# Results written into the memory of the split x, a step's four stores issued by ScalarE, and SyncE's gathers placed around the x loads

## The chip, the cores and the metric

The kernel runs on one core of one Trainium2 chip. The metric is the device time of one execution in microseconds. A core has five instruction streams that matter here: TensorE (PE, with its weight loads shown as PEld), VectorE (DVE), ScalarE (ACT), GpSimd (POOL) and SyncE (SP), and 16 DMA engines that all of them share. In this kernel SP computes nothing: it issues transfers.

## The reference, cut to what matters

The input x has 64 sequences of 64 tokens with 1024 features. Two layers are applied, each of which adds to x what an adapter pair and a feed-forward part with four small experts give:

```
x = x + ffn0(cond0(x))        cond: Bx = x @ B[id].T ; out = Bx @ A[id].T      (rank 16, one id per sequence)
x = x + ffn1(cond1(x))        ffn:  x @ W.T + b + sum_e softmax(router)_e * 2 * (x @ EA_e.T) @ EB_e.T
```

The adapter ids of a sequence choose among 8 (layer 0) and 64 (layer 1) adapters, so the adapter rows are gathered by values that are only known at run time.

## The kernel before, in words

**Tiling.** A step `g` is one of 8 groups of 8 sequences (512 tokens); x and the result are held as 128 partitions x 8 feature tiles x 512 tokens. One step's x is loaded in `CH` = 4 chunks of two feature tiles (512 KB each) into `xraw[par]`, where `par` alternates between two buffers. Every factor of a product is kept as a high part in fp32r and the low remainder: ScalarE copies the high part, DVE or GpSimd subtracts it for the low part, and TensorE runs three products. For x these parts are `xs_hi` and `xs_lo` (`xs[0]`, `xs[1]`): they hold only half of a step's tokens at a time, so they are written twice a step (`split_x`, half 0 and half 1).

**One step on TensorE.** `body(g)` begins with `ps_h` (from `bst`, the split B rows), then the selection `ps_s`, then the wide products W1 x A1 into three banks (`wide(0)`, `wide(1)`, and `wide(2)` in two pieces of four). Between the two pieces of `wide(2)` stands `turn()` (line 447): four transposes of `lp`, the weighted expert coefficients of layer 0, which DVE makes at the end of its `softmax(0)`. Then come `project(g + 1, 0)` and `project(g + 1, 1)`, which multiply the next step's split x, a second `turn()`, and the eight result tiles, each of which DVE adds to x (line 903) with a `d_out` signal.

**What DVE and ScalarE do in the first part of a step.** ScalarE: `h_and_k1(g)` (which first waits for a sum of DVE's), then `split_b(g + 1)` (four copies `bst_hi`), which waits until all 16 gathers of step g + 1 have landed (`gathered`), then `wide_high(0)` (`m1x_hi`), the copies of `ps_t`, and the first chunks of `split_x(g + 1)`. DVE, in the same order: `h_to_sbuf`, `k1_low`, `split_b` (four `bst_lo`), `wide_low(0)`, the `ps_t` parts, and `softmax(0)`, which ends with `lp` (line 855).

**SP's queue.** In `body(g)` SP prepares step g + 2: it waits until POOL has finished `split_a(g + 1)` (`a_lo`), gathers the eight sequences' adapter rows (for each sequence 64 KB at line 233 and 128 KB at line 235), and then for each chunk waits for `d_out`, stores the chunk (line 296), and loads the next x into the chunk before it (line 216) once that chunk's store has landed, since result and x share `xraw[par]`. The engines take instructions in program order; signals are semaphores. Steps 1 to 4 are two turns of a loop on SP, steps 0 and 5 to 7 are written out.

Of the kernel before, what the change touches and what calls it, by code (L numbers as in the profile page):

```python
# [29 lines left out]
P = 128  # L30
# [17 lines left out]
CH = 4  # L48
# [23 lines left out]
def two_layer_adapter_lora(nc, x_in, id0_row, all_ids, a0, b0_tab, ab1_tab, w0, w1, exp0, exp0_rows,  # L72
                           exp1_in, exp1_rows, bias, identity, marks, out):
    with ExitStack() as ctx:
        def sb(name, shape, dt=F32):
            return ctx.enter_context(nc.sbuf_tensor(name, shape, dt))

        def split(name, shape):

            return sb(name + "_hi", shape, F32R), sb(name + "_lo", shape, F32R)  # L80
# [8 lines left out]
        xraw = [sb(f"xraw{i}", [P, KT, TOK]) for i in range(2)]  # L89

        slots = [t[:, KC * i:KC * (i + 1), :].rearrange("p k t -> p (k t)") for t in xraw for i in range(CH)]
        xs = split("xs", [P, KT, HALF])
        abraw = sb("abraw", [P, GROUP, 2, SLOT])
        b0raw = sb("b0raw", [P, GROUP, SLOT])
        bst = split("bst", [P, KT, 4, HR_])
# [30 lines left out]
        bsum = sb("bsum", [P, KT])  # L126

        hr_hi, hr_lo = hr[:, :, 0, :], hr[:, :, 1, :]
        exp1_hi, exp1_lo = (w[:, :, D:WIDE] for w in w1s)

        zs = hsb[:].rearrange("p a n -> p (a n)")[:, 0:TT * FC].rearrange("p (j e c) -> p j e c", j=TT, e=EXP)
# [71 lines left out]
        def result_banks(last):  # L203

            return ps_d + [ps_p, ps_h] if last else ps_d

        def after_step(eng, signal, count):

            if not (isinstance(count, int) and count == 0):
                eng.wait_ge(signal, count)  # L210


        @block.sync
        def _(sp):
            def load_x(g, par, i):
                sp.dma_start(xraw[par][:, KC * i:KC * (i + 1), :],
                             x_in[bass.ds(g, 1), :, KC * i:KC * (i + 1), :]
                             .rearrange("a p k t -> p (a k) t")).then_inc(x_in_sem[i], 16)

            def values(first, count, limit):  # L220

                return nc.values_load_multi_w_load_instructions(
                    ids[0:1, bass.ds(first, count)], (mybir.EngineType.SP,), min_val=0, max_val=limit - 1)[1]

            def pick(g):

                return tuple(zip(values(g * GROUP, GROUP, ADAPT0), values(g * GROUP + SEQS, GROUP, SEQS)))

            def gather(picks, seqs):

                for b in seqs:
                    n0, n1 = picks[b]
                    sp.dma_start(b0raw[:, b, :],  # L233
                                 b0_tab[bass.ds(n0, 1)].rearrange("a p n -> p (a n)")).then_inc(gathered, 16)
                    sp.dma_start(abraw[:, b, :, :].rearrange("p a n -> p (a n)"),  # L235
                                 ab1_tab[bass.ds(n1, 1)].rearrange("a p n -> p (a n)")).then_inc(gathered, 16)

            sp.dma_start(ids[:], all_ids).then_inc(ids_in, 16)
            sp.dma_start(a0raw, a0).then_inc(a0_in, 16)
            for k in range(KT):  # L240
                sp.dma_start(w0raw[k], w0[k]).then_inc(w0_in[k], 16)
            sp.wait_ge(ids_in, 16)
            experts = values(2 * SEQS, EXP, 16)
            for e, n in enumerate(experts):
                sp.dma_start(exp0_raw[:, e, :], exp0[bass.ds(n, 1)].rearrange("a p n -> p (a n)")
                             ).then_inc(exp0_in, 16)
            picks = pick(0)
            sp.dma_start(ident[:], identity).then_inc(ident_in, 16)
            sp.wait_ge(a0_lo, 1)

            for i in range(CH):
                gather(picks, range(2 * i, 2 * i + 2))
                sp.wait_ge(w0_lo, i + 1)
                load_x(0, 0, i)
            sp.dma_start(mark[:], marks).then_inc(marks_in, 16)
            sp.dma_start(idi[:], id0_row).then_inc(marks_in, 16)
            for k in range(KT):
                if W1_SLOTS[k] in W1_SLOTS[:k]:

                    sp.wait_ge(w1_lo, max(j for j in range(k) if W1_SLOTS[j] == W1_SLOTS[k]) + 1)  # L260
                elif W1_SLOTS[k] == SPARE:
                    sp.wait_ge(m0t_done, 1)
                else:
                    sp.wait_ge(w0_lo, W1_SLOTS[k] + 1)
                sp.dma_start(w1raw[k], w1[k]).then_inc(w1_in[k], 16)
                if k == 2:
                    sp.dma_start(exp1_raw.rearrange("p k c -> p (k c)"), exp1_in).then_inc(exp1_sem, 16)
                    sp.dma_start(bia[:], bias).then_inc(exp1_sem, 16)
                    picks = pick(1)
                if k == 6:  # L270
                    sp.wait_ge(w1_lo, 4)
                    for e, n in enumerate(experts):
                        r0 = E0ROWS[0].start + e * ER
                        sp.dma_start(rows_raw[r0:r0 + ER, :],
                                     exp0_rows[bass.ds(n, 1)].rearrange("a r o -> (a r) o")
                                     ).then_inc(rows_in, 16)
                    sp.dma_start(rows_raw[E1ROWS[0], :], exp1_rows).then_inc(rows_in, 16)
            sp.wait_ge(b_lo, 4)
            sp.wait_ge(a_lo, 1)
            gather(picks, range(GROUP))  # L280
            sp.wait_ge(w1_lo, KT - 1)
            sp.wait_ge(w1_lo_pool, 1)
            for i in range(CH - 1):
                load_x(1, 1, i)
            sp.wait_ge(rows_lo, 2)
            load_x(1, 1, CH - 1)

            def body(g, par, last):
                ahead = not (isinstance(g, int) and g >= STEPS - 2)
                if ahead:  # L290
                    picks = pick(g + 2)
                    sp.wait_ge(a_lo, g + 2)
                    gather(picks, range(GROUP))
                for i in range(CH):
                    sp.wait_ge(d_out, KT * g + KC * (i + 1))
                    sp.dma_start(out[bass.ds(g, 1), :, KC * i:KC * (i + 1), :]
                                 .rearrange("a p k t -> p (a k) t"),
                                 xraw[par][:, KC * i:KC * (i + 1), :]).then_inc(stored[i], 16)
                    if ahead and i > 0:
                        sp.wait_ge(stored[i - 1], 16 * g + 16)  # L300
                        load_x(g + 2, par, i - 1)
                if ahead:
                    sp.wait_ge(stored[CH - 1], 16 * g + 16)
                    load_x(g + 2, par, CH - 1)

            steps(sp, body, 3)
            for i in range(CH):
                sp.wait_ge(stored[i], 16 * STEPS)


        @block.tensor
# [206 lines left out]
        def _(act):  # L518
            def copy(dst, src):
                return act.activation(dst, src, ACT.Copy)  # L520

            def split_x(g, par, half, chunks=range(CH)):
                n = 2 * g + half
                for i in chunks:
                    act.wait_ge(x_in_sem[i], 16 * g + 16)
                    if not (isinstance(n, int) and n == 0):
                        act.wait_ge(x_used, CH * n + (i + 1 - CH))
                    copy(xs[0][:, KC * i:KC * (i + 1), :],
                         xraw[par][:, KC * i:KC * (i + 1), half * HALF:(half + 1) * HALF]).then_inc(x_hi, 1)

# [83 lines left out]
            def body(g, par, last):  # L614
# [60 lines left out]
                if not last:  # L675
                    c0_high(g + 1)

            steps(act, body)


        @block.vector
        def _(dve):
# [113 lines left out]
            def body(g, par, last):  # L796
# [102 lines left out]
                banks = result_banks(last)  # L899

                for m in range(KT):
                    dve.wait_ge(d_done, KT * g + m + 1)
                    dve.scalar_tensor_tensor(out=xraw[par][:, m, :], in0=banks[m % len(banks)][:],  # L903
                                             scalar=bsum[:, m:m + 1], in1=xraw[par][:, m, :],
                                             op0=ALU.add, op1=ALU.add).then_inc(d_out, 1)
                    if not last and m == 1:
                        select(g + 1)
                    if not last and m == 2:
                        c0_low(g + 1)
# [5 lines left out]
        def _(pool):  # L915
            def low(dst, whole, high):
                return pool.tensor_tensor(dst, whole, high.bitcast(F32), ALU.subtract)  # L917

            def split_x(g, par, half, chunks):
                for i in chunks:  # L920
                    pool.wait_ge(x_hi, 2 * CH * g + CH * half + i + 1)
                    low(xs[1][:, KC * i:KC * (i + 1), :],
                        xraw[par][:, KC * i:KC * (i + 1), half * HALF:(half + 1) * HALF],
                        xs[0][:, KC * i:KC * (i + 1), :]).then_inc(x_lo, 1)
# [82 lines left out]
```

## Time and profile before

| | us |
|---|---|
| median of 3 runs | 353.43 (350.32 to 354.69) |
| the profiled execution | 353.02 |
| its span in the profile | 351.0 |
| TensorE busy | 326.0 (93%) |
| DVE busy | 246.0 (70%) |
| ScalarE busy | 149.8 (43%) |
| GpSimd busy | 89.9 (26%) |

The profile's page divides the span into 40 slices of 8.8 us. TensorE's digit there is 9 in nearly all slices after the first 80 us; the DMA digits swing between 0 and 9 within every step. In the chain that ended last, TensorE's work makes up 53% of the span. An engine's idle time matters only where TensorE waits for its result. Times below are from the span's start.

### The profile page before, as it was taken

To read this page: it belongs to the slowest core of one execution; us is meant where nothing else is said; L and a number is where in the kernel's file an instruction comes from. 1 tells how busy PE (TensorE), PEld (TensorE's weight loads), DVE (VectorE), ACT (ScalarE), POOL (GpSimd) and SP (SyncE) were. 2 spreads that over 40 slices of the span, in tenths; PEclk is the share of its full clock that TensorE was granted. 3 is DMA by queue.
4 is the path that set the end of the run, shared out by engine and by line. 5 is a ranking of instruction groups with operands and counts; after the bars stand their busy time and mean duration, and the time that the engine had idled before them with its cause. 6 is when DMAs were issued, how large, how long until landed. Compare 5 with 4: busy or idle time off the path is not lost.

```text
span 351.0 us, 6577 instructions
## 1 busy us (share of the span) xinstructions
PE 326.0 (93%) x2112; PEld 304.6 (87%) x2112; DVE 246.0 (70%) x496; ACT 149.8 (43%) x317; POOL 89.9 (26%) x61
## 2 busy tenths in 40 slices
PE   6998747889999999999999999999999999999975
PEld 5777647879999899989999999999999999999864
DVE  5925993797586867697668767775878586855554
ACT  5856833663065405550456036613562166203210
POOL 0014620184015500550046003620262026300000
PEclk9999898969999999999999999999999999999989
DMA  6889526611782078405950586048803780140005
GB/s 276 327 278 326 181 92 203 219 58 51 250 269 92 17 228 287 132 2 166 302 189 0 143 289 225 0 120 268 266 5 98 245 296 18 49 190 2 0 23 218
DMA packets 31525, 56.17 MB, mean 160 GB/s; under 512 B 3793, under 2 KB 21074, under 8 KB 31506
## 3 DMA queue, kind: packets, MB, share of 16 engines
q1 hardware_dynamic: 31506, 55.94, 47.9%
q8 instruction: 9, 0.15, 0.2%
q14 instruction: 10, 0.08, 0.1%
HBM read 39.15 MB, written 16.78 MB: 159 GB/s over the span
## 4 chain that ended last, share of the span: by engine, by line
PE 53%; issue 12%; DMA 10%; DVE 9%; POOL 6%; SPq 5%; ACT 4%; POOLq 0%; ACTq 0%; DVEq 0%
PE ps_d L316 12%; PE ps_d L318 12%; PE ps_d L317 12%; POOL xs_lo L917 5%; DMA xraw<-w 4%; DMA out<-xraw 3%; PE ps_h L323 3%; PE ps_p L316 2%; DVE k_lo L684 2%; PE ps_p L317 2%; PE ps_p L318 2%; PE ps_t L447 2%; DMA abraw<-ab_tab 2%; SPq L233 2%; SPq L235 2%
## 5 line engine op out<-in xcount | busy, mean ns | idle before, releaser
L917 POOL TENSOR_TENSOR xs_lo<-xraw,xs_hi 128x512 fp32r<-128x512 f32 x48 | 67.8, 1423 | 195.4 <-ACT xs_hi L520 195.3
L316 PE MATMUL ps_d<-w1s_hi,a1s_hi 128*128 128x384 f32 (+1 forms) x216 | 72.7, 337 | 1.8 <-DVE w1s_lo L684 1.8
L318 PE MATMUL ps_d<-w1s_hi,a1s_lo 128*128 128x384 f32 (+1 forms) x216 | 70.2, 325 | 0.0
L317 PE MATMUL ps_d<-w1s_lo,a1s_hi 128*128 128x384 f32 (+1 forms) x216 | 70.2, 325 | 0.0
L903 DVE SCALAR_TENSOR_TENSOR xraw<-ps_d,bsum,xraw 128x512 f32<-128x512 f32 x62 | 46.3, 750 | 27.5 <-PE ps_d L318 27.5
L520 ACT ACTIVATE xs_hi<-xraw 128x512 fp32r<-128x512 f32 x64 | 38.4, 624 | 17.6 <-DMA xraw<-x_in 11.1
L316 PEld LDWEIGHTS ps_d<-w1s_hi,a1s_hi 128*128 128x128 f32 x216 | 41.1, 190 | 3.9 <-DVE w1s_lo L684 3.8
L316 PE MATMUL ps_p<-xs_hi,bst_hi 128*128 128x256 f32 x128 | 39.4, 307 | 3.4 <-POOL xs_lo L917 2.5
L317 PEld LDWEIGHTS ps_d<-w1s_lo,a1s_hi 128*128 128x128 f32 x216 | 41.1, 190 | 0.0
L318 PEld LDWEIGHTS ps_d<-w1s_hi,a1s_lo 128*128 128x128 f32 x216 | 41.0, 190 | 0.0
L317 PE MATMUL ps_p<-xs_lo,bst_hi 128*128 128x256 f32 x128 | 37.8, 295 | 0.0
L318 PE MATMUL ps_p<-xs_hi,bst_lo 128*128 128x256 f32 x128 | 37.7, 295 | 0.0
L316 PE MATMUL ps_d<-k_hi,m1x_hi 128*128 128x256 f32 x124 | 35.8, 289 | 1.4 <-DVE k_lo L684 1.4
L520 ACT ACTIVATE hsb<-hsb 128x32 f32<-128x32 f32 x8 | 1.8, 228 | 82.3 <-DVE hsb L704 82.3
L318 PE MATMUL ps_d<-k_hi,m1x_lo 128*128 128x256 f32 x124 | 35.6, 287 | 0.0
L317 PE MATMUL ps_d<-k_lo,m1x_hi 128*128 128x256 f32 x124 | 35.5, 286 | 0.0
L316 PEld LDWEIGHTS ps_p<-xs_hi,bst_hi 128*128 128x128 f32 x128 | 26.3, 205 | 4.9 <-issue 2.0
L684 DVE TENSOR_TENSOR m1x_lo<-ps_d,m1x_hi 64x384 fp32r<-64x384 f32 (+1 forms) x48 | 24.4, 509 | 5.9 <-ACT m1x_hi L520 5.1
L316 PEld LDWEIGHTS ps_d<-k_hi,m1x_hi 128*128 128x128 f32 x124 | 24.0, 194 | 3.6 <-DVE k_lo L684 1.6
L317 PEld LDWEIGHTS ps_p<-xs_lo,bst_hi 128*128 128x128 f32 x128 | 26.3, 206 | 0.0
L318 PEld LDWEIGHTS ps_p<-xs_hi,bst_lo 128*128 128x128 f32 x128 | 26.2, 204 | 0.0
L520 ACT ACTIVATE m1x_hi<-ps_d 64x384 fp32r<-64x384 f32 (+1 forms) x48 | 21.3, 444 | 11.0 <-PE ps_d L318 10.6
(156 smaller groups left out, 691.8 us busy)
## 6 DMA issues: line engine op xcount, KB each, us to landing
xraw<-x_in SPq DMA_DIRECT2D x32, 512.0 KB, 5.0
out<-xraw SPq DMA_DIRECT2D x32, 512.0 KB, 3.6
xraw<-w SPq DMA_DIRECT2D x16, 512.0 KB, 6.5
abraw<-ab_tab SPq DMA_DIRECT2D x64, 128.0 KB, 2.1
b0raw<-b_tab SPq DMA_DIRECT2D x64, 64.0 KB, 1.9
b0raw<-a SPq DMA_DIRECT2D x1, 512.0 KB, 3.7
lp<-exp SPq DMA_DIRECT2D x4, 69.0 KB, 7.5
cm<-exp_in SPq DMA_DIRECT2D x1, 144.0 KB, 5.3
```

The source lines that it names most:

```text
L233: sp.dma_start(b0raw[:, b, :], b0_tab[bass.ds(n0, 1)].rearrange("a p n -> p (a n)")).then_inc(gathered, 16)
L235: sp.dma_start(abraw[:, b, :, :].rearrange("p a n -> p (a n)"), ab1_tab[bass.ds(n1, 1)].rearrange("a p n -> p (a n)")).then_inc(gathered, 16)
L316: pe.matmul(acc, lh, rh, start=first, stop=False, skip_group_check=True)
L317: pe.matmul(acc, lh, rl, start=False, stop=False, skip_group_check=True)
L318: return pe.matmul(acc, ll, rh, start=False, stop=final, skip_group_check=True)
L323: pe.matmul(acc, high, right.rearrange("p a n -> p (a n)"), start=first, stop=False, skip_group_check=True)
L447: mm = pe.transpose(ps_t[:, j * P:(j + 1) * P], lp[:, at:at + P], ident[:])
L520: return act.activation(dst, src, ACT.Copy)
L684: return dve.tensor_tensor(dst, whole, high.bitcast(F32), ALU.subtract)
L903: dve.scalar_tensor_tensor(out=xraw[par][:, m, :], in0=banks[m % len(banks)][:], scalar=bsum[:, m:m + 1], in1=xraw[par][:, m, :], op0=ALU. ...
L917: return pool.tensor_tensor(dst, whole, high.bitcast(F32), ALU.subtract)
```

## The change

Three things are altered. **First**, the result tiles get memory of their own: `done`, 16 KB per partition, allocated over the address of `xs_hi` and `xs_lo`. Its four chunks lie as two over `xs_hi` and two over `xs_lo`. DVE's line that adds the result now writes `done` in place of `xraw`. So an x chunk of step g + 2 can be loaded when DVE has read the old x (`d_out`), without waiting for a store; and what writes `xs` next (ScalarE for `xs_hi`, GpSimd for `xs_lo`, the first half of the following step's `split_x`) first waits for the stores of what lies there. **Second**, the four stores are issued by ScalarE, at the end of its `body`. **Third**, SP issues the first four gathers, then chunk 0 of x, two gathers, chunk 1, two gathers, chunk 2, chunk 3.

```
+        xs_at = nc.sbuf_base
         xs = split("xs", [P, KT, HALF])
+        done_ = nc.alloc_sbuf_tensor_at("done", [P, KT * TOK], F32, offset=xs_at)
...
+        done = [done_[:, KC * TOK * i:KC * TOK * (i + 1)] for i in range(CH)]
...
+        def stored_by(g):
+            return 0 if isinstance(g, int) and g == 0 else 16 * g - 16
...
@@ sync, body
-                    gather(picks, range(GROUP))
-                for i in range(CH):
-                    sp.wait_ge(d_out, KT * g + KC * (i + 1))
-                    sp.dma_start(out[bass.ds(g, 1), :, KC * i:KC * (i + 1), :]
-                                 .rearrange("a p k t -> p (a k) t"),
-                                 xraw[par][:, KC * i:KC * (i + 1), :]).then_inc(stored[i], 16)
-                    if ahead and i > 0:
-                        sp.wait_ge(stored[i - 1], 16 * g + 16)
-                        load_x(g + 2, par, i - 1)
-                if ahead:
-                    sp.wait_ge(stored[CH - 1], 16 * g + 16)
-                    load_x(g + 2, par, CH - 1)
+                    gather(picks, range(HSEQ))
+                    for i in range(CH):
+                        sp.wait_ge(d_out, KT * g + KC * (i + 1))
+                        load_x(g + 2, par, i)
+                        if i < 2:
+                            gather(picks, range(HSEQ + 2 * i, HSEQ + 2 * i + 2))
...
@@ scalar, split_x
+                    if half == 0:
+                        after_step(act, stored[i // KC], stored_by(g))
...
@@ scalar, end of body
+                for i in range(CH):
+                    act.wait_ge(d_out, KT * g + KC * (i + 1))
+                    act.dma_start(out[bass.ds(g, 1), :, KC * i:KC * (i + 1), :]
+                                  .rearrange("a p k t -> p (a k t)"), done[i]).then_inc(stored[i], 16)
...
@@ vector, results
+                    if last and m % KC == 0:
+                        dve.wait_ge(stored[m // KC], 16 * g)
                     dve.wait_ge(d_done, KT * g + m + 1)
-                    dve.scalar_tensor_tensor(out=xraw[par][:, m, :], in0=banks[m % len(banks)][:],
+                    dve.scalar_tensor_tensor(out=done[m // KC][:, m % KC * TOK:(m % KC + 1) * TOK],
+                                             in0=banks[m % len(banks)][:],
...
@@ gpsimd, split_x
+                    if half == 0:
+                        after_step(pool, stored[KC + i // KC], stored_by(g))
```

The waits for the end of the last stores move from SP to ScalarE. Nothing changes on TensorE.

On SP, in the loop's first turn before, this is the end of the gathers (`b0raw`, `abraw`) and what follows them, with the stores (`out<-xraw1`) and the x loads (`xraw1<-x_in`); ISA and REGISTER_ALU rows prepare addresses and wait values:

```order
L233 DMA b0raw<-b0_tab 128x128
L235 ISA
L235 DMA abraw<-ab1_tab 128x256
L295 ISA
L296 ISA
L296 DMA out<-xraw1 128x1024
L295 REGISTER_ALU
L296 ISA
L296 DMA out<-xraw1 128x1024
L300 ISA
L216 ISA
L216 DMA xraw1<-x_in 128x1024
```

And this is the same stretch of SP now, from the fourth sequence's gathers over the first x load and the fifth and sixth:

```order
L243 DMA abraw<-ab1_tab 128x256
L303 ISA
L224 ISA
L224 DMA xraw1<-x_in 128x1024
L241 ISA
L241 DMA b0raw<-b0_tab 128x128
L243 ISA
L243 DMA abraw<-ab1_tab 128x256
```

Four of a step's eight pairs of gathers now stand behind one or two x loads; none did before. On ScalarE, the last of the four stores at a step's end and the beginning of the next step, as it is now; the rows of lines 681 and 682 are new, and before this the copy `c0s_hi` was followed by the address row and the copy `hsb`:

```order
L681 REGISTER_ALU
L682 ISA
L682 DMA out<-done_49 128x1024
L543 REGISTER_ALU
L520 ACTIVATE hsb<-hsb 128x32
L520 ACTIVATE k1_hi<-ps_s 128x512
L534 ISA
L520 ACTIVATE bst_hi<-abraw 128x4x8x16
```

The row of line 534 is the address of the `split_b` copies, which wait for the gathers; it stands where it stood.

## Rows read from the trace of the kernel before

**Rows 1.** Windows, one steady step: us, busy of each engine, PEclk, DMA share, GB/s

```profile
184.70:220.90 36.20, 35.89 (x249) 34.22 (x249) 26.59 (x57) 15.16 (x36) 10.70 (x8) 1.00 0.49 159
```

**Rows 2.** Timeline of ScalarE: start, us, instruction [idle before]; a step's first copy

```profile
133.75 0.23 ACT L520 ACTIVATE hsb<-hsb 128x32 f32<-128x32 f32 x1 [11.75 <-DVE hsb L704]
...
170.57 0.23 ACT L520 ACTIVATE hsb<-hsb 128x32 f32<-128x32 f32 x1 [11.76 <-DVE hsb L704]
...
206.78 0.23 ACT L520 ACTIVATE hsb<-hsb 128x32 f32<-128x32 f32 x1 [11.75 <-DVE hsb L704]
```

**Rows 3.** Timeline of ScalarE in that step, from split_b to the last first-half chunk

```profile
207.53 0.62 ACT L520 ACTIVATE bst_hi<-abraw 128x512 fp32r<-128x512 f32 x1
...
210.42 0.99 ACT L520 ACTIVATE m1x_hi<-ps_d 64x384 fp32r<-64x384 f32 x2 [0.71 <-PE ps_d L318]
...
212.21 1.14 ACT L520 ACTIVATE xs_hi<-xraw 128x512 fp32r<-128x512 f32 x2
...
219.04 0.63 ACT L520 ACTIVATE xs_hi<-xraw 128x512 fp32r<-128x512 f32 x1 [0.33 <-DMA xraw<-x_in]
```

**Rows 4.** Timeline of VectorE in that step, behind its split_b

```profile
210.94 1.15 DVE L684 TENSOR_TENSOR m1x_lo<-ps_d,m1x_hi 64x384 fp32r<-64x384 f32 x2 [0.18 <-ACT m1x_hi L520]
212.34 0.29 DVE L684 TENSOR_TENSOR c0s_lo<-ps_t,c0s_hi 128x128 fp32r<-128x128 f32 x1 [0.25 <-ACT hls_hi L520]
...
216.38 0.29 DVE L855 TENSOR_TENSOR lp<-hsb,lg 128x128 f32<-128x128 f32 x1
```

**Rows 5.** Waits, 193 to 229.2 us, then 112 to 330 us: total us, times, longest

```profile
PEld ps_t L447 <- DVE lp L855: 0.2, 1, 0.2
...
ACT xs_hi L520 <- DMA xraw<-x_in: 5.2, 8, 1.6
```

**Rows 6.** Timeline of VectorE, a step's first two and last result tiles

```profile
195.16 1.47 DVE L903 SCALAR_TENSOR_TENSOR xraw<-ps_d,bsum,xraw 128x512 f32<-128x512 f32 x2 [0.79 <-PE ps_d L318]
...
203.68 0.75 DVE L903 SCALAR_TENSOR_TENSOR xraw<-ps_d,bsum,xraw 128x512 f32<-128x512 f32 x1 [0.67 <-PE ps_d L318]
```

**Rows 7.** Timeline of SyncE's queue: first and last gather, first and later x loads

```profile
193.96 0.34 SPq L233 DMA_DIRECT2D b0raw<-b_tab  x1
...
201.69 0.33 SPq L235 DMA_DIRECT2D abraw<-ab_tab  x1
...
205.28 0.35 SPq L216 DMA_DIRECT2D xraw<-x_in  x1
...
211.53 2.98 SPq L216 DMA_DIRECT2D xraw<-x_in  x2
```

**Rows 8.** The page's DMA issues: KB each, median us from issue to landing

```profile
xraw<-x_in SPq DMA_DIRECT2D x32, 512.0 KB, 5.0
...
abraw<-ab_tab SPq DMA_DIRECT2D x64, 128.0 KB, 2.1
b0raw<-b_tab SPq DMA_DIRECT2D x64, 64.0 KB, 1.9
```

**Rows 9.** Windows without engine columns: us, PEclk, DMA share, GB/s

```profile
3.00:14.00 11.00, 1.00 1.02 412
...
19.00:25.00 6.00, 1.00 0.90 278
...
194.00:197.10 3.10, 1.00 0.40 122
...
208.00:213.00 5.00, 1.00 0.97 361
```

**Rows 10.** The chain that ended last: start, us, what; the first step's last gather

```profile
24.60 5.62 DMA abraw<-ab_tab
```

**Rows 11.** Windows of TensorE alone: us, PE busy, PEclk, DMA share, GB/s

```profile
57.00:58.00 1.00, 0.00 (x0) 1.00 0.66 202
...
69.00:71.00 2.00, 0.12 (x1) 1.00 0.35 94
72.00:78.00 6.00, 5.31 (x24) 0.50 0.04 15
```

More of the change, by code:

```diff
@@ L292, in body @@
                     sp.wait_ge(a_lo, g + 2)
-                    gather(picks, range(GROUP))
-                for i in range(CH):
-                    sp.wait_ge(d_out, KT * g + KC * (i + 1))
-                    sp.dma_start(out[bass.ds(g, 1), :, KC * i:KC * (i + 1), :]
-                                 .rearrange("a p k t -> p (a k) t"),
-                                 xraw[par][:, KC * i:KC * (i + 1), :]).then_inc(stored[i], 16)
-                    if ahead and i > 0:
-                        sp.wait_ge(stored[i - 1], 16 * g + 16)
-                        load_x(g + 2, par, i - 1)
-                if ahead:
-                    sp.wait_ge(stored[CH - 1], 16 * g + 16)
-                    load_x(g + 2, par, CH - 1)
+                    gather(picks, range(HSEQ))
[4 more added lines that the diff above has]
+                            gather(picks, range(HSEQ + 2 * i, HSEQ + 2 * i + 2))
             steps(sp, body, 3)
-            for i in range(CH):
-                sp.wait_ge(stored[i], 16 * STEPS)
         @block.tensor
@@ L676, in body @@
                     c0_high(g + 1)
+                for i in range(CH):
+                    act.wait_ge(d_out, KT * g + KC * (i + 1))
+                    act.dma_start(out[bass.ds(g, 1), :, KC * i:KC * (i + 1), :]
+                                  .rearrange("a p k t -> p (a k t)"), done[i]).then_inc(stored[i], 16)
             steps(act, body)
+            for i in range(CH):
+                act.wait_ge(stored[i], 16 * STEPS)
         @block.vector
```

## The prediction, made before the changed kernel was run

> **What bounds the kernel now.** I read the windows of one steady step first, then the waits, then the timelines of ScalarE, VectorE and SyncE over that step, and last the windows of the DMA engines. In a steady step TensorE is busy for 35.89 of 36.20 us at the full clock [rows 1]: a step is as long as TensorE's work, and the change takes none of it away. What can be won is only what TensorE waits for in connection with x. The first copies of two steps are 36.82 us apart (133.75 to 170.57), those of the next 36.21 (170.57 to 206.78) [rows 2]. The long one is the step in which x came late. ScalarE waited for x for 5.2 us in 8 places [rows 5], but most of that lies under TensorE's work: apart from the 0.6 us of the long step nothing of it reaches a step's length. So the gain to be had is about 0.7 us in all.
>
> What can be lost hangs on a narrower chain. DVE ends `lp` at 216.38 + 0.29 = 216.67 [rows 4], and TensorE waits for it before `turn()`, by 0.2 us already [rows 5]. Behind its four `bst_lo`, DVE idles only 0.18 us before `m1x_lo` and 0.25 us before `c0s_lo` [rows 4]. So when `split_b` comes late by more than 0.43 us, `lp` is late by the rest, and TensorE, which takes its instructions in order, stands still for as long. `split_b` starts at 207.53, directly behind ScalarE's earlier work and with no wait for a DMA [rows 3]: the gathers are in memory then. The last is issued at 201.69 [rows 7] and takes 2.1 us to land [rows 8], so they are there at about 203.8, 3.7 us early. That slack is what the change spends.
>
> **The change, part by part.**
>
> *The results' memory.* DVE's 64 result instructions keep shape and operands from the same memories; I cost them at nothing (0.75 us each as now [rows 6]). In the last step DVE has four more waits, for stores issued a step ago: nothing.
>
> *ScalarE issues 32 stores.* No row shows a DMA issue on ScalarE. SP's issue of one takes 0.33 to 0.35 us in the rows of its queue [rows 7], the slowest kind there 1.49 (2.98 for two, which held a wait in it). The last result tile ends at 203.68 + 0.75 = 204.43 [rows 6], and ScalarE's next work starts at 206.78 [rows 2], after 11.75 us of idling. Behind the last wait stands one issue: done at 204.8, or at 205.9 with the dear price. ScalarE's copies behind it are on time either way: 0, and not below 0, since nobody waits for these instructions. Queued behind the waits for `d_out` are exactly those copies, and the gap is the cover.
>
> *The new waits of ScalarE and GpSimd for the stores.* They stand before the first-half chunks of x, the earliest at 212.21 [rows 3], and the stores of the lower half of `done` are issued from 196.7 on (195.16 + 1.47 [rows 6]). At 212.21 ScalarE needs the first store and GpSimd, just behind it, the third; both are issued before the last gather, which lands at about 209.3 (worked out below): 0. In the last step the stores are issued by ScalarE behind the same last tile as by SP now: 0.
>
> *x earlier.* SP issues x chunk 0 at about 198.3 and not at 205.28, the last two at about 203.7 and 204.6 and not from 211.53 on [rows 7]. The needs are at 212.21 for the first and 219.04 for the last [rows 3]. The late x disappears: -0.7 us in all.
>
> *The gathers later.* This is the term that decides. SP's gathers start at 193.96 and go out at 0.52 us each (201.69 - 193.96 over 15). In the new order four pairs are out at 198.1, x chunk 0 follows, two pairs, chunk 1, two pairs: the last gather goes out at about 203.2, 1.5 us later than now. In front of it or beside it the engines now have eight pairs (192 KB each [rows 8], 1.57 MB), two x loads and, from 196.7 on, three stores (512 KB each, 2.62 MB): 4.19 MB. Before, only the gathers were there. Until 197.1 the trace of today moves 122 GB/s x 3.1 us = 0.38 MB [rows 9]. The other 3.81 MB take 9.2 us at 412 GB/s, the best rate of a queue of large transfers; 10.6 us at 361, the rate of x loads and stores mixed; 13.7 us at 278, the rate of gathers mixed with x loads [rows 9]. I take 350 GB/s, since two thirds of the bytes are large transfers: 10.9 us, to 208.0. From the last byte to the signal I add 1.3 us, an estimate: of a gather's 2.1 us [rows 8], 0.33 is the issue and about 0.5 its own bytes. The gathers are all there at 209.3. A second row agrees in kind: in the first step SP issued gathers and x loads in just such a mix, and the last gather, issued at 24.60, landed 5.62 us later [rows 10]; 203.2 + 5.6 is 208.8, without stores beside it.
>
> So `split_b` starts at 209.3 and not 207.53, 1.77 us late; less 0.43 of slack TensorE loses 1.34 us. The lateness comes back in every step, because SP's start hangs on `a_lo` and on `d_out`, which move with TensorE. The gathers of body 0 to 5 feed `split_b` of six steps: 6 x 1.34 = +8.0 us. Between its ends the term is 0 (412 GB/s: 206.3 + 1.3 = 207.6, within the slack; a gain is excluded, as `split_b` does not wait for gathers now) and 6 x 4.1 = +24.9 us (278 GB/s: 210.8 + 1.3 = 212.1, 4.57 late, less 0.43). What is late next is nothing new: with TensorE shifted, all later waits of the step shift too.
>
> **The sum.** -0.7 + 8.0 = +7.3 us on the profiled execution's 353.02, so 360.3; the median of the runs shown is 0.4 us above that execution, so I write 360.7. That is 2.1% over the median, and 2%, about what a measurement of this kernel can tell from no change, is 7.1 us.
>
> **How the DMA engines share their time** is not in this trace: all transfers are SP's. The sum above serves bytes as they come. The Trainium skill (DMA: Bandwidth & Descriptors, section Queues, rings and completion order) says that each of two issuing engines has its own ring on each DMA engine and that a DMA engine takes turns between rings that have work, a packet at a time. No run here shows it; by that rule the sum would be the second rival's, +18.8 us. The same page (Issuing engines are not separate DMA queues) says that issuing on two engines adds no bandwidth, which speaks against this change; the sum already counts all transfers against one rate.
>
> **Rivals.**
>
> *The gathers still land in time* (not slower). Place: ScalarE's `split_b`; price: nothing but the 0.7 us won. It decides below a landing at 208.0, that is at 395 GB/s or more after 197.1. For it: 412 GB/s has been moved for 11 us on end [rows 9], and a store beside a load may fill what a load alone leaves idle. Against it: the mixed rate of 361, and the 5.62 us of [rows 10]. Time: 353.4 - 0.7 = 352.7.
>
> *The stores take half of the engines.* From 197.1 SP's own queue holds 1.19 MB of gathers and 1.05 MB of x up to its last gather; at half of 350 GB/s that is 12.8 us, to 209.9, and the signal at 211.2: 3.67 late, 3.24 lost, six times 19.5, less 0.7: +18.8, so 372.2. For it: the stores' queue has work nearly all that time. Against it: the two queues carry much the same number of bytes, so that first-come and half-and-half differ only by the fourth store and by the time it starts.
>
> *TensorE's clock falls after each new stall.* Between 69 and 71 us TensorE is busy for 0.12 us, and its granted clock is 0.50, the 1.2 GHz level, from 72 to 78 [rows 11]. Against it: it idled from 57 to 58 us at a clock of 1.00 [rows 11], and a stall of 1.3 us is nearer to that. Were each of six stalls followed by 3 us, half of what [rows 11] show, at half the clock, 1.5 us of work would be lost each time: +9.0 on top of 7.3, so 369.7.
>
> *A gain that tells.* It would need 7.1 us, while all idle time of TensorE in seven steady steps is some 7 x 0.31 us [rows 1] and the late x. I see no mechanism.
>
> **How the numbers follow.** Gathers late by the sum's mechanism 0.45, spread from +1 to +16 us around +7.3, about 0.25 of it over 2% and 0.20 under; in time 0.27; half of the engines 0.13; the clock 0.12; a telling gain 0.03. Slower 0.25 + 0.13 + 0.12 = 0.50, within 2% 0.20 + 0.27 = 0.47, faster 0.03. Since the cases of both kinds hold most of the chance, the likeliest one's own range is 354 to 369. The full range goes down to 351, the case in time with the spread of the runs (350.32 to 354.69), and up to 374, which takes in the half share and the clock; the 24.9 us end stays out, with less than 0.1.
>
> **What would show it.** In the changed trace: ScalarE's first `bst_hi` of steps 1 to 6 with idle time put down to a gather's DMA, about 1.8 us (right), or none (the first rival); TensorE's wait before line 447 for `lp` at 1.3 to 1.6 us a step and not 0.2; steps 37.5 us long and not 36.2; `xs_hi` waiting for x no more; the DMA share near 1 from 197 to 212 us of that step, and then low. A granted clock under 1.00 in the steady steps would speak for the third rival. I am wrong if the step keeps 36.2 us, or if ScalarE's `hsb` copy comes late behind its stores.

## The result, and the profile after

The changed kernel takes 381.64 us (median of 4 runs, 380.24 to 385.74) against 353.37 us: ratio 1.083, 95% interval 1.072 to 1.094. It is 28 us slower. The forecast of 360.7 us had the direction, but the time lies above the range of 351 to 374.

The profiled execution took 380.24 us with a span of 378.1. The page's lines of TensorE and of the DMA engines by slice:

```profile
PE 332.4 (88%) x2112; PEld 309.6 (82%) x2112; DVE 242.8 (64%) x496; ACT 149.5 (40%) x317; POOL 88.8 (23%) x61
DMA  7897437308900493008900690049301960032005
```

TensorE runs the same 2112 products and is busy 6.4 us longer, with 88% of the span instead of 93%. The DMA engines now alternate between full slices and empty ones: a step's transfers have been pushed together. ScalarE's timeline over the same part of a step as in [rows 2, 3] (start, us, instruction, idle before it and who ended it), one step further on in the program's time:

```profile
211.15 8.17 ACTq L682 DMA_DIRECT2D out<-done  x4
221.14 0.23 ACT L520 ACTIVATE hsb<-hsb 128x32 f32<-128x32 f32 x1 [11.75 <-DVE hsb L713]
...
225.70 0.63 ACT L520 ACTIVATE bst_hi<-abraw 128x512 fp32r<-128x512 f32 x1 [3.71 <-DMA abraw<-ab_tab]
```

The four stores end before `hsb`, which again follows after 11.75 us of idling: issuing them costs ScalarE's work nothing. `split_b`, which followed `hsb` and `k_hi` without a wait in [rows 3], now waits 3.71 us for gathers. The waits of the six steps behind the start, 90 to 345 us (total, times, longest):

```profile
ACT bst_hi L520 <- DMA abraw<-ab_tab: 24.3, 6, 5.0
PE ps_t L447 <- DVE lp L864: 19.9, 6, 4.3
```

Every one of six `split_b` is late, by 24.3 us together, and TensorE stands still before `turn()` for 19.9 us of it. SyncE's queue in this step, as in [rows 7]:

```profile
208.35 0.34 SPq L241 DMA_DIRECT2D b0raw<-b_tab  x1
...
212.59 0.55 SPq L224 DMA_DIRECT2D xraw<-x_in  x1
...
215.43 0.86 SPq L243 DMA_DIRECT2D abraw<-ab_tab  x1
216.54 0.39 SPq L224 DMA_DIRECT2D xraw<-x_in  x1
...
218.91 0.33 SPq L243 DMA_DIRECT2D abraw<-ab_tab  x1
219.49 0.91 SPq L224 DMA_DIRECT2D xraw<-x_in  x2
```

The last gather goes out 10.56 us after the first (218.91 - 208.35) and not 7.73 as before. It has landed 17.35 us after the first was issued (225.70). What the DMA engines did meanwhile (us, PEclk, DMA share, GB/s):

```profile
208.35:212.00 3.65, 1.00 0.41 127
212.00:217.00 5.00, 1.00 0.93 261
217.00:225.70 8.70, 1.00 1.04 400
```

And what TensorE did behind the late `split_b` (us, PE busy, PEclk, DMA share, GB/s):

```profile
221.20:231.20 10.00, 9.96 (x67) 1.00 0.60 235
231.20:234.30 3.10, 0.16 (x1) 1.00 0.00 0
234.30:237.60 3.30, 3.30 (x13) 0.52 0.00 0
237.60:261.90 24.30, 23.99 (x169) 1.00 0.43 136
```

It is dense, then idle for 3 us, then works 3.3 us at a granted clock of 0.52, the 1.2 GHz level, then dense again at 2.4 GHz.

**Where the 28 us are.** Over the six steps from the second `hsb` copy to the last, the time went from 217.94 us (97.42 to 315.36 in the trace of before) to 246.56 (97.38 to 343.94): +28.6. The windows of TensorE over exactly these six steps, before and then after, tell the kinds apart (us, PE busy, PEclk, DMA share, GB/s):

```profile
97.42:315.36 217.94, 215.58 (x1484) 1.00 0.48 156
```

```profile
97.38:343.94 246.56, 224.83 (x1484) 0.96 0.38 136
```

The same 1484 products in the records took 224.83 us instead of 215.58: 9.3 us for the slower clock. TensorE's idle time grew from 2.36 to 21.73, by 19.4: the stalls are 19.9, and elsewhere it idles 0.5 us less. The two make up the 28.6. Outside these steps the new span is 1.5 us shorter.

### The profile page after: what moved, and what is told of

It is laid out like the page before. It is cut to its first block, busy times and chain, and to the rows that moved or that the text cites. A ratio compares the mean times of both kernels' runs of the same rounds, so it can differ in the third digit from the quotient of the medians.

```text
span 378.1 us, 6659 instructions
## 1 busy us (share of the span) xinstructions
PE 332.4 (88%) x2112; PEld 309.6 (82%) x2112; DVE 242.8 (64%) x496; ACT 149.5 (40%) x317; POOL 88.8 (23%) x61
## 4 chain that ended last, share of the span: by engine, by line
issue 20%; PE 19%; DMA 16%; SPq 15%; POOL 12%; DVE 9%; ACT 7%; POOLq 0%; ACTq 0%
DMA abraw<-ab_tab 13%; POOL xs_lo L929 9%; SPq L241 6%; SPq L243 6%; PE ps_d L316 4%; PE ps_d L318 4%; PE ps_d L317 4%; DMA xraw<-w 4%; ACT bst_hi L520 3%; POOL a1s_lo L929 3%; SPq L224 2%; DVE w1s_lo L693 2%; DVE xs_lo L693 1%; DVE bst_lo L693 1%; PE ps_p L316 1%
## 5 line engine op out<-in xcount | busy, mean ns | idle before, releaser
L316 PE MATMUL ps_d<-w1s_hi,a1s_hi 128*128 128x384 f32 (+1 forms) x216 | 76.5, 354 | 3.2 <-DVE w1s_lo L693 3.2
L318 PE MATMUL ps_d<-w1s_hi,a1s_lo 128*128 128x384 f32 (+1 forms) x216 | 73.3, 339 | 0.0
L317 PE MATMUL ps_d<-w1s_lo,a1s_hi 128*128 128x384 f32 (+1 forms) x216 | 73.2, 339 | 0.0
L914 DVE SCALAR_TENSOR_TENSOR done<-ps_d,bsum,xraw 128x512 f32<-128x512 f32 x62 | 46.1, 749 | 26.1 <-PE ps_d L318 26.1
L316 PEld LDWEIGHTS ps_d<-w1s_hi,a1s_hi 128*128 128x128 f32 x216 | 44.1, 204 | 5.7 <-DVE w1s_lo L693 5.4
L317 PEld LDWEIGHTS ps_d<-w1s_lo,a1s_hi 128*128 128x128 f32 x216 | 43.8, 203 | 0.0
L318 PEld LDWEIGHTS ps_d<-w1s_hi,a1s_lo 128*128 128x128 f32 x216 | 43.4, 201 | 0.0
L520 ACT ACTIVATE xs_hi<-xraw 128x512 fp32r<-128x512 f32 x64 | 37.1, 620 | 13.3 <-PE ps_p L318 8.2
L447 PE MATMUL ps_t<-ident,lp 128*128 128x128 f32 x64 | 11.4, 306 | 21.0 <-DVE lp L864 21.0
L693 DVE TENSOR_TENSOR bst_lo<-abraw,bst_hi 128x512 fp32r<-128x512 f32 x16 | 12.6, 786 | 24.6 <-ACT bst_hi L520 24.6
L447 PEld LDWEIGHTS ps_t<-ident,lp 128*128 128x128 f32 x64 | 7.8, 150 | 23.4 <-DVE lp L864 23.3
```

The lines of the kernel that those rows point to most:

```text
L316: pe.matmul(acc, lh, rh, start=first, stop=False, skip_group_check=True)
L317: pe.matmul(acc, lh, rl, start=False, stop=False, skip_group_check=True)
L318: return pe.matmul(acc, ll, rh, start=False, stop=final, skip_group_check=True)
L447: mm = pe.transpose(ps_t[:, j * P:(j + 1) * P], lp[:, at:at + P], ident[:])
L693: return dve.tensor_tensor(dst, whole, high.bitcast(F32), ALU.subtract)
L914: dve.scalar_tensor_tensor(out=done[m // KC][:, m % KC * TOK:(m % KC + 1) * TOK], in0=banks[m % len(banks)][:], scalar=bsum[:, m:m + 1], i ...
```

## The experiments

All ratios are to the kernel before, timed beside each kernel on the same chip; its median was 351.5 to 353.4 us on the chips used, so the ratios compare better than the times. "Wait" is what ScalarE waited for gathers in the six steps, in all; "stall" is TensorE's idle time before `turn()` in the same six steps. The kernel before has none of either there.

| | time, us | ratio (95%) | wait | stall |
|---|---|---|---|---|
| the change | 381.64 | 1.083 (1.072 to 1.094) | 24.3 | 19.9 |
| gathers first | 352.23 | 0.999 (0.996 to 1.002) | 1.0 | 0.3 |
| order of the change, stores on SyncE | 364.41 | 1.028 (1.021 to 1.035) | 14.2 | 10.0 |
| no stores | 351.68 | 0.998 (0.995 to 1.001) | 1.0 | none |
| x chunks 2 and 3 held | 380.03 | 1.078 (1.072 to 1.083) | 24.1 | 19.7 |
| filler products | 373.40 | 1.061 (1.056 to 1.066) | 24.9 | 4.2 |
| fourth store late | 366.78 | 1.043 (1.038 to 1.048) | 16.4 | 12.1 |
| third and fourth store late | 356.90 | 1.013 (1.008 to 1.018) | 8.9 | 4.8 |
| x chunk 1 behind the gathers | 361.80 | 1.030 (1.023 to 1.037) | 11.0 | 6.8 |
| own memory alone | 352.96 | 1.005 (1.001 to 1.009) | none | 1.4 |
| order alone | 384.18 | 1.093 (1.084 to 1.102) | 26.6 | 21.6 |

### Gathers first

```
-                    gather(picks, range(HSEQ))
+                    gather(picks, range(GROUP))
                     for i in range(CH):
                         sp.wait_ge(d_out, KT * g + KC * (i + 1))
                         load_x(g + 2, par, i)
-                        if i < 2:
-                            gather(picks, range(HSEQ + 2 * i, HSEQ + 2 * i + 2))
```

> The changed kernel with one part undone: SyncE issues all eight pairs of gathers ahead of the four x loads, as before the change; results' own memory and the stores on ScalarE stay. Theory (the x loads in front of the last gathers make them late): split_b waits for no DMA or under 0.5 us, steps are 36.2 us long, the time is 352 to 355 us. Rival (the stores on a second queue take the engines from the gathers, whatever SyncE's order): split_b still waits 1.5 us or more in each of six steps, and the time is above 362 us.

Measured 352.23 us, as expected. ScalarE waited once in six steps, for 1.0 us where under 0.5 was expected:

```profile
ACT bst_hi L518 <- DMA abraw<-ab_tab: 1.0, 1, 1.0
```

With the order of before, results' own memory and ScalarE's stores cost nothing that can be measured, and they win nothing either. Putting the gathers back ahead of the x loads takes the whole 28 us away. The rival, that the second queue by itself takes the engines from the gathers, is out.

### The order of the change with the stores on SyncE

```
                     gather(picks, range(HSEQ))
-                    for i in range(CH):
-                        sp.wait_ge(d_out, KT * g + KC * (i + 1))
+                for i in range(CH):
+                    sp.wait_ge(d_out, KT * g + KC * (i + 1))
+                    sp.dma_start(out[...], done[i]).then_inc(stored[i], 16)
+                    if ahead:
                         load_x(g + 2, par, i)
                         if i < 2:
                             gather(picks, range(HSEQ + 2 * i, HSEQ + 2 * i + 2))
```

and no stores on ScalarE.

> The changed kernel with the stores issued by SyncE again, each ahead of the x load of its chunk and of the two pairs of gathers behind it; results' own memory and the place of the gathers stay, so that all transfers are in one queue. If what stands ahead of the last gathers is what counts, as bytes, they are late here too, since a queue in order has two stores, two x loads and all gathers up to there: a wait of 2 to 4 us before split_b and 370 to 383 us. If the sharing between two queues costs more than the order (what is issued later on the other queue overtakes the gathers), the wait falls under 2 us and the time under 368 us.

Measured 364.41 us, and a wait of 14.2 us, 2.4 a step:

```profile
ACT bst_hi L523 <- DMA abraw<-ab_tab: 14.2, 6, 3.5
```

The result falls between the two expectations: the wait is in the first one's band, the time in the second's. Both statements hold in part. The order costs 10.0 us of stalls also in a single queue; with the stores on ScalarE there are another 9.9. In the single queue the third and fourth store are issued behind the last gather; from ScalarE they go out beside the gathers.

### No stores

```
                     act.wait_ge(d_out, KT * g + KC * (i + 1))
+                    if last:
+                        act.dma_start(out[...], done[i]).then_inc(stored[i], 16)
...
```

The waits for these stores in ScalarE's and GpSimd's `split_x` and in DVE's last step go too. The results of steps 0 to 6 are left out, so this kernel only measures.

> The changed kernel without the stores of steps 0 to 6 (only the last step's result reaches memory); its waits for d_out stay. It measures what the stores add beside the gathers. Theory: two x loads alone still lie ahead of the last gathers, but with 2.1 MB less to move the gathers land within 1 us of when split_b is due: time 350 to 358 us. Rival (the x loads ahead are enough): split_b still waits 2 us or more, 365 us or more.

Measured 351.68 us; three of six steps wait, 1.0 us in all:

```profile
ACT bst_hi L520 <- DMA abraw<-ab_tab: 1.0, 3, 0.5
```

Two x loads ahead of the last gathers just about use up the slack. Together with the gathers-first run: neither the order without stores nor the stores without the order does harm; it takes both. With the stores the wait is 24.3 - 1.0 = 23.3 us longer, 3.9 us a step for four stores of 512 KB, three of which my sum had counted. It is a lower bound, since gathers that land before `split_b` is due show in no wait.

### x chunks 2 and 3 held until the gathers have landed

```
                         sp.wait_ge(d_out, KT * g + KC * (i + 1))
+                        if i == 2:
+                            sp.wait_ge(gathered, 16 * 2 * GROUP * (g + 3))
                         load_x(g + 2, par, i)
```

> The changed kernel, but SyncE issues x chunks 2 and 3 only when all gathers of the step have landed. They are issued behind the gathers, so if transfers were served as they come, nothing changes for the gathers: the wait before split_b stays at 3.3 to 5 us and the time at 380 us or a little more. Rival (transfers issued later delay the last gathers' signal too): the wait shrinks by 1 us or more a step and the time falls to 372 us or less.

Measured 380.03 us, wait 24.1: the theory. What is issued behind the last gather in its own queue does not delay it. The windows of one step, from the first gather's issue to the last one's landing (us, PEclk, DMA share, GB/s), and two single microseconds of the same stretch:

```profile
209.30:213.00 3.70, 1.00 0.46 129
213.00:218.00 5.00, 1.00 0.95 271
218.00:226.60 8.60, 1.00 0.88 336
...
224.00:225.00 1.00, 1.00 0.93 370
225.00:226.00 1.00, 1.00 0.34 118
```

With nothing else issued, the bytes moved by the landing can be counted: 0.48 + 1.36 + 2.89 = 4.72 MB. All gathers (1.57), two x loads (1.05) and four stores (2.10) are 4.72. So by the time the last gather's signal comes, the fourth store has been moved as well, though it was issued at the same time as that gather (in the changed kernel's trace ScalarE's four issues of a step end at 219.32, SyncE's last gather goes out at 218.91). The windows count bytes and not whose they are: whether the gather's own bytes came behind the store's, or only its signal did, they do not tell.

### The fourth store issued a step later

```
+            def store(g, i):
+                act.dma_start(out[...], done[i]).then_inc(stored[i], 16)
...
                 if not last and not first:
                     split_b(g + 1)
+                if not first:
+                    act.wait_ge(d_out, KT * g)
+                    for i in (3,):
+                        store(g - 1, i)
...
                 for i in range(CH):
-                    act.wait_ge(d_out, KT * g + KC * (i + 1))
+                    if i not in (3,) or last:
+                        act.wait_ge(d_out, KT * g + KC * (i + 1))
+                        store(g, i)
```

> The changed kernel, but ScalarE issues the fourth store of a step only in the next step, behind its split_b copies, so that it cannot move beside the gathers. Theory (the stores' queue gets its turn at once, so that even the fourth store, issued just before the last gather, is served ahead of it; each 512 KB beside the gathers costs 1.5 us at 350 GB/s): the wait before split_b falls from 3.3 to 5.0 us to 1.8 to 3.5, stalls of TensorE fall by 1.2 to 1.5 us a step, and with fewer falls of the clock the time is 366 to 373 us. Rival (only what is issued ahead of the last gathers on SyncE's own queue counts beside the first three stores): the wait keeps its length, time 379 to 383.

Measured 366.78 us. The wait fell by 24.3 - 16.4 = 7.9 us, 1.3 a step:

```profile
ACT bst_hi L520 <- DMA abraw<-ab_tab: 16.4, 6, 3.4
```

The expectation holds in all its numbers. The fourth store is issued no earlier than the last gather, and yet it delays it: what another queue has to move beside the gathers counts as if it stood ahead of them. SyncE's last gather goes out as long after the first as in the change (10.62 us on the mean of the six steps, 10.57 there), so all of the 1.3 us lies behind its issue.

TensorE's clock is told by this run too. It fell in two of the six steps, one of them behind a stall of 2.0 us; with the stores on SyncE it stayed up behind one of 2.8 us. The stall and the time behind it, first in this run, then in that one (us, PE busy, PEclk, DMA share, GB/s):

```profile
223.00:226.00 3.00, 1.04 (x8) 1.00 0.00 0
226.70:230.00 3.30, 3.30 (x12) 0.50 0.00 0
```

```profile
145.00:148.00 3.00, 0.24 (x2) 1.00 0.00 0
148.00:152.00 4.00, 4.00 (x27) 1.00 0.01 2
```

### The third and the fourth store late

The same with `for i in (2, 3)`.

> As the run before, but the third and the fourth store both wait until the gathers have landed. Theory: 1.05 MB less beside the gathers, 3.0 us earlier, so a wait of 0.3 to 2 us before split_b, no or few falls of the clock, 354 to 362 us. Rival as before: 372 us or more.

Measured 356.90 us; the wait is 8.9 us in six steps, 1.2 us a step less again:

```profile
ACT bst_hi L520 <- DMA abraw<-ab_tab: 8.9, 6, 2.4
```

The granted clock in the window of these six steps is 1.00. Time and clock are as expected, and so are five of the six waits (1.1 to 1.6 us; the sixth is 2.4). Against the change the gathers come 2.6 us a step earlier and not 3.0.

This run sheds light on the one with the stores on SyncE, where two stores and two x loads are likewise issued ahead of the last gathers. The wait is 5.3 us less here, in two queues, than there in one. There SyncE has to issue the stores as well, and its last gather goes out 11.33 us after the first on the mean of the six steps, here 10.37. So a second queue is no harm by itself; harmful are the third and the fourth store, which it lets move beside the gathers.

### x chunk 1 behind the gathers

```
                         load_x(g + 2, par, i)
-                        if i < 2:
-                            gather(picks, range(HSEQ + 2 * i, HSEQ + 2 * i + 2))
+                        if i == 0:
+                            gather(picks, range(HSEQ, GROUP))
```

> The changed kernel with only x chunk 0 among the gathers: four pairs, chunk 0, four pairs, then chunks 1 to 3. Stores as in the change. Theory (each 512 KB ahead of the last gather costs 1.5 us, a load as much as a store): the wait before split_b falls by 1.2 to 1.8 us to 1.8 to 3.5, time 366 to 373 us. Rival (a load in the gathers' own queue holds them up more than its bytes): the wait falls under 1 us and the time under 360.

Measured 361.80 us, below the 366 to 373 expected; the wait fell by 13.3 us, 2.2 a step where 1.2 to 1.8 was expected:

```profile
ACT bst_hi L520 <- DMA abraw<-ab_tab: 11.0, 6, 2.9
```

It is neither theory's number, and nearer to the first. A load ahead in the gathers' own queue costs more than a store beside them, 2.2 us against 1.3 and 1.2. SyncE's issue is a part of that: in the changed kernel gathers behind an x load took up to 0.86 us to issue (the row at 215.43) where each took 0.33 to 0.34 in [rows 7]. The traces divide the 2.2 us. Here is one step of this run, from SyncE's first and last gather to `split_b`:

```profile
200.36 0.34 SPq L241 DMA_DIRECT2D b0raw<-b_tab  x1
...
210.02 0.33 SPq L243 DMA_DIRECT2D abraw<-ab_tab  x1
```

```profile
215.14 0.63 ACT L520 ACTIVATE bst_hi<-abraw 128x512 fp32r<-128x512 f32 x1 [1.11 <-DMA abraw<-ab_tab]
```

On the mean of the six steps the last gather goes out 10.05 us after the first (10.57 in the change) and `split_b` starts 15.55 us after it (17.70). So 0.5 us is issue, and 1.6 us lies behind it, near the 1.5 of the theory.

### Filler products in TensorE's stall

```
+                if not last and not (isinstance(g, int) and g == 0):
+                    for _ in range(12):
+                        pe.matmul(ps_p[:], m0s[0][:, 0:P], m0s[1][:, 0:TOK], start=True, stop=True,
+                                  skip_group_check=True)
                 pe.wait_ge(l_done, 2 * g + 1)
```

> The changed kernel with 12 products that nobody reads (128x512, operands that are constant after the set-up, into the bank ps_p, which is free there) on TensorE in steps 1 to 6, between the first half of wide(2) and the wait for lp: about 2.9 us of work at the full clock, in a place where TensorE idles 2.6 to 4.3 us. The gathers' lateness stays. Theory (each stall is followed by a stretch at 1.2 GHz that costs 1.5 to 2 us): the clock stays at 1.00 in all or nearly all of the steady steps and the time falls by 6 to 10 us, to 371 to 376 us. Rival (the clock's fall costs nothing to speak of beside the stall): within 2 us of the changed kernel's 381.6.

Measured 373.40 us. The gathers are as late as in the change (24.9 us), yet TensorE's window over the six steps shows the full clock:

```profile
96.00:335.00 239.00, 232.91 (x1559) 1.00 0.40 141
```

Six steps take 238.43 us (from `hsb` at 96.20 to 334.63) where they took 246.56: 8.1 us less for work that nobody reads, against the 9.3 us that the busy time had shown. So the clock's share of the loss is real, and most of it can be avoided without touching the cause of the stalls; the gathers' lateness, the larger share, remains.

### The results' own memory alone

All eight pairs first, and then store and load by turns on SyncE: the diff of the second run with `gather(picks, range(GROUP))` and without the two inner gathers.

> The results' own memory alone: all eight pairs of gathers first, then SyncE issues store 0, x 0, store 1, x 1 and so on in one queue, no load waiting for a store. Theory: the gathers have nothing ahead of them and land in time; x is early; 351 to 354 us, no measurable difference from the kernel before or from the run with the stores on ScalarE. Rival (the x loads, no longer held by the stores' landings, crowd the gathers even when issued behind them): a wait before split_b of 1 us or more and 358 us or more.

Measured 352.96 us, ratio 1.005 (1.001 to 1.009); no wait for a gather in the six steps. The rival is out. Half a per cent slower is just outside the interval, but within what I called no difference.

### The order alone, in the kernel before

```
                 if ahead:
-                    gather(picks, range(GROUP))
+                    gather(picks, range(HSEQ))
                 for i in range(CH):
...
                     if ahead and i > 0:
                         sp.wait_ge(stored[i - 1], 16 * g + 16)
                         load_x(g + 2, par, i - 1)
+                        if i < 3:
+                            gather(picks, range(HSEQ + 2 * i - 2, HSEQ + 2 * i))
```

> The kernel before with the order alone changed: four pairs of gathers, store 0, store 1, x 0, two pairs, store 2, x 1, two pairs, store 3, x 2, x 3, each x load behind the landing of its chunk's store as before. The last gathers now also stand behind two landings of stores, about 3 us apart from their issue. Theory (order decides, whoever issues the stores): SyncE's last gather goes out 4 to 6 us later than before (behind the landing of store 1 and the issue of x 1), lands 2 to 5 us behind that, so the wait before split_b is 3 to 6 us and the time 372 to 392 us. Rival (the order hurts only beside loads and stores that run unheld): a wait under 1 us, within 5 us of the kernel before.

Measured 384.18 us, as slow as the whole change, with a wait of 4.4 us a step. SyncE's queue in one step:

```profile
248.64 0.34 SPq L233 DMA_DIRECT2D b0raw<-b_tab  x1
...
252.88 1.26 SPq L296 DMA_DIRECT2D out<-xraw  x2
255.86 0.35 SPq L216 DMA_DIRECT2D xraw<-x_in  x1
...
259.09 0.33 SPq L216 DMA_DIRECT2D xraw<-x_in  x1
...
261.81 0.33 SPq L235 DMA_DIRECT2D abraw<-ab_tab  x1
```

Here the last gather goes out 13.17 us after the first and not 7.73 as before, since SyncE waits for stores in between, and has landed 5.3 us later (a little over the 2 to 5 expected). In the change it goes out after 10.56 us and has landed 6.8 later. So here most of the lateness is issue, and in the change most of it is the time to landing. Own memory without the order costs nothing. What the order costs depends on what else moves: 9% in the kernel before, 8% with own memory and stores on ScalarE, 3% with own memory and stores on SyncE, nothing without stores.

No version that writes all results beat the kernel before. The best, with the gathers first, equals it.

## Why the prediction was right or wrong, point by point

**The bound and the chain: right.** TensorE's work sets a step, and the chain from the gathers over `split_b`, `softmax(0)` and `lp` to `turn()` is where the time was lost. Waits of 3.33 to 5.01 us became stalls of 2.6 to 4.3: the slack taken off is 0.7 us, where I had 0.43.

**Stores on ScalarE, results' memory, new waits for stores, last stores: right.** All cost nothing ("gathers first", 0.999).

**x earlier, -0.7 us: right in what it does, not borne out as a gain.** In the six steps x is waited for no more. But with the gathers first these steps take 218.02 us, against 217.94 before; only without stores are they shorter, 217.16. Why the first of these does not win the 0.7 was not tried.

**The gathers later: the step that failed, by its size.** The sum put 8.0 us on the gathers' lateness (1.77 us a step, less the slack) and nothing on the clock. The stalls are 19.9 us (4.05 a step, less the slack), inside the term's bounds of 0 and 24.9 but above the spread that I gave a chance. I took 350 GB/s for what the engines move; after 212 us they moved 1.31 + 3.48 = 4.79 MB in 13.7 us, 349 GB/s. The rate was right. Wrong were the bytes that have to move before the last gather is in: I served them "as they come", three stores and two loads, 4.19 MB. In the run with chunks 2 and 3 held it was 4.72 MB, the fourth store included, and taking that store away gave back 1.3 us a step. At the predicted rate 0.52 MB more is 1.5 us, so 16.8 us from first gather to landing; I had 15.34, the trace 17.35. For what is left SyncE's own issue is a candidate, 10.56 us for the gathers' row instead of 9.24; that was not shown. A landing 2.0 us later adds to a lateness of only 1.77, so it more than doubles the term: the predicted term was a small difference between two large numbers, and every error in the larger went into it whole.

**The rival "half of the engines": its number was the better one.** It gave a landing at 211.2, 17.24 us after the first gather, against 17.35 in the step shown and 17.70 on the mean of six. Its stall of 3.24 us a step meets the 3.3 partly by luck: its lateness was 0.4 us too small and its slack 0.3 too small. The Trainium skill (DMA: Bandwidth & Descriptors, section Queues, rings and completion order) has a DMA engine take turns between the rings with work. The runs agree as far as they go: a store issued together with the last gather was moved before its signal came (4.72 MB), and moving it away brought the gathers forward. How long a turn is they do not show. I had written against this rival that first-come and half-and-half differ only by the fourth store; that was so, and the fourth store was worth 7.9 us of waiting. That the engines are shared by halves is not shown; that the fourth store counts is.

**The rival "the clock falls": it came on top.** I had priced it at 9.0 us and gave it 0.12; it cost 9.3. I had judged it from a stall of 1.3 us. With 3 us and more the nearer rows were those of 69 to 71 and 72 to 78 us [rows 11]. The fall and the lateness are one case and not two: a longer stall makes the fall likelier. Five of the six steps show it; the one without is the shortest, 38.89 us, with the shortest stall, 2.6. The length of the stall alone does not decide: over all runs the clock fell behind every stall of 2.9 us and more, behind some of 2.0 to 2.6 (two of 2.0 and 2.6 us in the run with the fourth store late), and not behind one of 2.8 (stores on SyncE).

**The range.** Both rivals' additions together (19.5 + 9.0 - 0.7 = 27.8 us) give 381.2, and 381.64 was measured. That it is so near is partly luck: six falls of 1.5 us were priced, and there were four that cost about 1.6 us and one of 2.7. I had let either in up to 374, but not the two together, though the first makes the second likely.

## What to carry to other kernels

Issue a transfer that something needs early in the next step ahead of those with slack, and keep large ones of any engine's queue out of the same microseconds: here each 512 KB ahead of the gathers or beside them made them 1.2 to 2.2 us later, while x had nothing to win. Before moving a transfer later, work out its slack from its issue and its time to landing, since a transfer that is early shows in no wait. Where a new stall of the matmul engine is likely, price the slower clock behind it with the stall and not as a case of its own.

## What the runs showed of the hardware

- The median time to landing of the gathers of 128 and 64 KB was 2.1 and 1.9 us [rows 8]; in the changed kernel, with the same sizes and number:

```profile
abraw<-ab_tab SPq DMA_DIRECT2D x64, 128.0 KB, 4.1
b0raw<-b_tab SPq DMA_DIRECT2D x64, 64.0 KB, 3.3
```

- The issue of a store on ScalarE took 0.34 to 0.38 us where its queue's rows show one alone, as on SyncE.
- The stores and loads of a step reached 400 GB/s for 8.7 us when both queues had them to move, but 261 GB/s in the 5 us before, where gathers and large transfers mixed at a share of 0.93.
- TensorE idle for about 3 us was followed by 3.3 us at a clock of 0.52 (the windows of the changed kernel above). In the step with the shortest stall it idled 2.6 us (5.00 - 2.38) and the clock stayed at 1.00, but in the run with the fourth store late it fell to 0.50 behind 2.0 us of idling. The first one's window, us, PE busy, PEclk, DMA share, GB/s:

```profile
192.00:197.00 5.00, 2.38 (x16) 1.00 0.00 0
```

  Twelve products in the stall kept the clock at 1.00 over all six steps.
